# The rotated convolution of every image on 32x32 tiles, with ScalarE turning half of the sums back

## The chip, the cores and the metric

The program runs on one core of a Trainium2 chip. The metric is device time in microseconds, from one launch to its end; the reference and the outputs are float32.

## What is computed

A network of four residual layers over x, (4, 256, 64, 64). Layer 0 is a deformable convolution (its samples are gathered rows of a table), layer 1 a grouped 3x3 convolution whose kernels are rotated by an angle that each image gives itself, layer 2 linear attention, layer 3 a quantised grouped convolution. The change touches layer 1 alone:

```python
B, C, H, W = x.shape                       # 4, 256, 64, 64
G, Cg = (base_kernel.shape[0], base_kernel.shape[1])      # 8 groups of 32 channels
pooled = x.mean(axis=(2, 3))
h = jax.nn.relu(pooled @ ap_w1.T + ap_b1)
angles = jnp.tanh(h @ ap_w2.T + ap_b2) * (math.pi / 4)
rot = jax.vmap(jax.vmap(_rotate_one), in_axes=(None, 0))(base_kernel, angles)
w = rot.reshape(B * C, Cg, K, K)
out = jax.lax.conv_general_dilated(x.reshape(1, B * C, H, W), w, ..., feature_group_count=B * G)
m = jax.nn.relu(pooled @ meta_w1.T + meta_b1)
mod = jax.nn.sigmoid(m @ meta_w2.T + meta_b2)
return feat * mod[:, :, None, None]
```

Before the convolution the image is normalised; its result, times `mod`, is added to the image.

## The kernel before

The images are worked off in turn, and each goes through A (first part of layer 0), F (its second part), L1, L2 and, last of all, L3. Images are named b = 0 to 3. A channel image is 128 partitions by 4096 elements, in two halves (k = 0, 1), and is worked in 8 chunks of 512 columns; PSUM `PS` has 8 banks of 128x512.

**The stream.** Layer 0's samples of the next image are fetched while the phases of this image run. A unit is one of 4 groups of one of 32 tiles: GpSimd issues 9 indirect gathers (L482) into one of the 4 slots of `ring`, after a wait on `ring_free`; VectorE multiplies the slot by the weights (TENSOR_TENSOR, L1700), adds up (TENSOR_REDUCE, L1706) and so frees it. At the first unit of a tile VectorE also moves the weights (COPY, L1689). In the program of VectorE the units are laid between the instructions of the phase: `stream.begin(part, gi, i)` takes those of one iteration (2 tiles, that is 8 units, in L1 of images 0 and 1; 1 tile in that of image 2, part "L1 last"; none in that of image 3), `stream.give(1, 4)` lays down a quarter of them, `stream.finish()` the rest. So L1 holds 32, 32, 16 and 0 units. GpSimd runs ahead of VectorE by at most the four slots, from one phase into the next.

**L1 of images 0 to 2.** TensorE builds the rotated kernels (36 products `PS<-cb,params`), VectorE copies them, masked, into a zeroed 128x128 matrix for each tap (`wa_sb`, four copies on L2156; the zeroing, L2111, is done for image 0 only). A loop of 4 iterations then does 2 chunks in each: 18 float32 matmuls 128x128x512 a chunk (9 taps, 2 halves; each shows as two records in the trace) into two banks; VectorE adds the chunk to the image (2 instructions on L2166) and takes its statistics (2 on L2171), with a quarter of the iteration's units ahead of each chunk and one behind. Semaphore `lC` counts chunks that TensorE has done, `lX` those that VectorE has taken; `room(pe, "lX", n)` lets TensorE be two chunks ahead. ScalarE has nothing to do in this loop, and waits at the barrier behind it.

**L1 of image 3**, where no units are left, is packed: the eight groups lie apart on the array, so 16 matmuls of 32x32 run on 16 tiles at a time. A batch n = 0 to 3 (`quad`, `k`) is 4 chunks of one half, 144 matmuls, 288 records. Tile (r, j) writes the sums of rows r to partitions (r + j) % 4 of bank 2j + k, so chunk j comes out turned by j x 32 partitions. VectorE turns it back as it adds: 1, 4, 2 and 4 instructions (L2183), then 4 statistics (L2188).

Of the kernel before, what the change touches and what calls it, by code (L numbers as in the profile page):

```python
# [28 lines left out]
P = 128  # L29
# [106 lines left out]
def network_kernel(nc, x, par, wa, wr, wf, wq, w3, out):  # L136
    ctx = ExitStack()
    with ctx:
# [222 lines left out]
        def packed(n):  # L361

            return START + (B - 1) * CHUNKS + n
# [490 lines left out]
        def _(pe):  # L854
# [211 lines left out]
            def L1(b):  # L1066
# [22 lines left out]
                def l1(i):  # L1089
                    for h in range(2):  # L1090
                        n, c = i * 2 + (b * CHUNKS + h), i * 2 + h
                        room(pe, "lX", n)
                        for k in range(KC):
                            for tap in range(K2):
                                at = R_SIZE + (k * K2 + tap) * P
                                last = mm(PS[:, 2 * h + k, :].rearrange("p (r x) -> p r x", x=W), wseg(wa_sb, at, P),
                                          padded(k, c, tap // 3, tap % 3), tap == 0, tap == K2 - 1)
                        last.then_inc(sem("lC"), 1)

                def l1_packed(quad, k):  # L1100

                    if quad:
                        pe.wait_ge(sem("lX"), packed(k + 1))
                    for tap in range(K2):
                        for j in range(4):
                            for r in range(4):
                                to = (r + j) % 4
                                at = R_SIZE + (k * K2 + tap) * CG
                                rs, os_ = slice(r * CG, (r + 1) * CG), slice(to * CG, (to + 1) * CG)
                                last = mm(rows(PS[os_, 2 * j + k, :]), wa_sb[rs, at:at + CG],  # L1110
                                          padded(k, quad * 4 + j, tap // 3, tap % 3)[rs], tap == 0, tap == K2 - 1,
                                          tile_position=(r * CG, to * CG), skip_group_check=True)
                    last.then_inc(sem("lC"), 1)

                if b < B - 1:
                    loop(l1)
                else:
                    for quad in range(2):
                        for k in range(KC):
                            l1_packed(quad, k)  # L1120
# [184 lines left out]
        def _(act):  # L1305
# [164 lines left out]
            def L1(b):  # L1470
# [19 lines left out]
                barrier()  # L1490
                barrier()
# [182 lines left out]
        def _(dve):  # L1674
# [415 lines left out]
            def L1(b, gi):  # L2090
# [17 lines left out]
                lt = wseg(wa_sb, R_SIZE, KC * K2 * P)  # L2108
                if b == 0:

                    link(vec.memset(lt, 0.0))  # L2111
# [16 lines left out]
                dve.wait_ge(sem("l1_hats"), b + 1)  # L2128
# [20 lines left out]
                sums = PS[:, 2:4, 0:K2 * CG].rearrange("p k (t o) -> p k t o", t=K2)  # L2149
                if b == B - 1:  # L2150
                    last = vec.tensor_copy(lt[:, 0:KC * K2 * CG].rearrange("p (k n) -> p k n", k=KC), PS[:, 2:4, 0:K2 * CG])
                else:
                    lt4 = lt.rearrange("p (k t o) -> p k t o", k=KC, t=K2)
                    for q in range(P // CG):
                        r_ = slice(q * CG, (q + 1) * CG)
                        last = vec.tensor_copy(lt4[r_, :, :, r_], sums[r_])  # L2156
                link(last)
                barrier()

                def l1(i):  # L2160
                    for h in range(2):
                        n, c = i * 2 + (b * CHUNKS + h), i * 2 + h
                        stream.give(1, 4)
                        done(dve, "lC", n)
                        for k in range(KC):
                            last = vec.scalar_tensor_tensor(out=chunk_of(img1, k, c), in0=PS[:, 2 * h + k, :], scalar=mod[:, k:k + 1],  # L2166
                                                            in1=chunk_of(img1, k, c), op0=ALU.mult, op1=ALU.add)
                        last.then_inc(sem("lX"), 1)
                        done(dve, "lX", n)
                        for k in range(KC):  # L2170
                            vec.bn_stats(seg(stats, c * 6 + k * 48, 6), chunk_of(img1, k, c))  # L2171
                        stream.give(1, 4)
                def l1_packed(quad, k):

                    n = quad * KC + k
                    dve.wait_ge(sem("lC"), packed(n + 1))
                    for j in range(4):
                        img = chunk_of(img1, k, quad * 4 + j)
                        width = (P, CG, 2 * CG, CG)[j]
                        for first in range(0, P, width):  # L2180
                            to = slice(first, first + width)
                            at = (first + j * CG) % P
                            last = vec.scalar_tensor_tensor(out=img[to], in0=PS[at:at + width, 2 * j + k, :],  # L2183
                                                            scalar=mod[to, k:k + 1], in1=img[to], op0=ALU.mult, op1=ALU.add)
                    last.then_inc(sem("lX"), 1)
                    dve.wait_ge(sem("lX"), packed(n + 1))
# [3 lines left out]
                if b < B - 1:  # L2190
                    chunks("L1" if gi != B - 1 else "L1 last", gi, 0, l1)
                else:
                    for quad in range(2):
                        for k in range(KC):
                            l1_packed(quad, k)
# [385 lines left out]
```

## Time and profile before

| | |
|---|---|
| median of 3 runs | 8428.0 us (8407.72 to 8446.78) |
| profiled execution, own time | 8406.53 us |
| its span, first to last instruction | 8404.7 us |
| mean granted TensorE clock | 0.711 |
| busy: TensorE, VectorE, ScalarE, GpSimd | 3952.7, 5151.7, 1232.6, 4440.0 us |
| loop of L1, image 0 | 2719.82 to 3094.4: 374.6 us |
| image 1 | 4593.96 to 4969.5: 375.5 us |
| image 2 | 6447.44 to 6654.8: 207.3 us |
| image 3, packed | 7853.30 to 7907.0: 53.7 us |

A loop's start is the first instruction of its phase behind the barrier, its end the first one behind the next barrier. All times inside a phase are us from the span's start.

### The profile page before, as it was taken

The numbers are of one execution on the slowest core, as the hardware profiler recorded it, in microseconds if no ns is written. First come the engines' busy times: TensorE is split into PE (matmuls) and PEld (weight loads), VectorE is DVE, ScalarE is ACT, GpSimd is POOL, SyncE is SP. The second block draws the span as 40 slices with busy tenths as digits, with TensorE's granted clock in tenths as the row PEclk, the third lists the DMA queues.
The fourth block names the chain that finished last, engine by engine and source line by source line (L and its number), as shares of the span: only waits on it lengthen the run. The fifth ranks groups of instructions, "written<-read, shape, count | busy, mean of one in ns | idle before, by whom it ended". The sixth has DMA issues, their size and how long they took to land.

```text
span 8404.7 us, 44163 instructions
## 1 busy us (share of the span) xinstructions
PE 3952.7 (47%) x11246; PEld 2022.5 (24%) x11246; DVE 5151.7 (61%) x4233; ACT 1232.6 (15%) x1846; POOL 4440.0 (53%) x4684
## 2 busy tenths in 40 slices
PE   6133241341365535442555435442565544428797
PEld 3121121221122213221222113221222222213453
DVE  6667668576566646664666646654666665553556
ACT  1000100001111001111111001111110011112246
POOL 2666656666565655565665655565666555650000
PEclk8566665675687657766787667766787777669899
DMA  4442533534333322244333322244333223441128
GB/s 130 129 128 87 158 113 123 151 109 136 111 107 96 99 85 87 90 153 161 115 96 102 99 81 91 88 159 150 116 113 95 76 89 96 151 149 42 43 99 236
DMA packets 511085, 953.74 MB, mean 113 GB/s; under 512 B 252032, under 2 KB 300928, under 8 KB 494848
## 3 DMA queue, kind: packets, MB, share of 16 engines
q0 software_dynamic: 221184, 604.27, 23.3%
q1 hardware_dynamic: 289792, 348.19, 12.9%
q8 instruction: 47, 0.77, 0.0%
q14 instruction: 62, 0.51, 0.0%
HBM read 791.89 MB, written 160.24 MB: 113 GB/s over the span
## 4 chain that ended last, share of the span: by engine, by line
issue 30%; another core or an unknown queue 26%; DVE 17%; PE 17%; ACT 4%; POOL 3%; DMA 2%; DVEq 1%; SPq 1%; ACTq 0%; POOLq 0%
PE PS L859 16%; DVE ring L1700 6%; DVE dbuf L1706 3%; ACT img L1310 3%; POOL ring L482 3%; DVE PS L1882 1%; DMA img<-d_dram 1%; DVE cb L1767 1%; DVEq L384 1%; DVE img L2067 1%; ACT cb L1310 0%; DVE stats L1762 0%; DVE img L2183 0%; PE PS L1176 0%
## 5 line engine op out<-in xcount | busy, mean ns | idle before, releaser
L482 POOL DMA_INDIRECT ring<-table,idx_stage x4608 | 4422.2, 960 | 3021.7 <-DVE dbuf L1706 1550.4
L1706 DVE TENSOR_REDUCE dbuf<-ring 128x64 f32<-128x2304 f32 x512 | 2071.1, 4045 | 109.6 <-issue 79.8
L859 PE MATMUL PS<-img,wb_sb 128*128 128x512 f32 (+1 forms) x3264 | 1646.0, 665 | 989.4 <-issue 401.9
L1700 DVE TENSOR_TENSOR ring<-ring,PS 128x2304 f32<-128x2304 f32 x480 | 1222.6, 2547 | 119.6 <-DMA ring<-table,idx_stage 101.4
L859 PE MATMUL PS<-img,wa_sb 128*128 (+2 forms) x2908 | 944.3, 635 | 624.2 <-issue 459.7
L859 PEld LDWEIGHTS PS<-img,wb_sb 128*128 128x128 f32 x3264 | 688.3, 215 | 1913.2 <-issue 1692.9
L859 PEld LDWEIGHTS PS<-img,wa_sb 128*128 128x128 f32 (+2 forms) x2908 | 385.2, 166 | 1153.7 <-issue 1123.1
L859 PE MATMUL PS<-wb_sb,img 128*128 128x512 f32 x512 | 344.1, 837 | 518.3 <-ACT cb L1310 221.5
L859 PE MATMUL PS<-wa_sb,cb 128*128 128x256 f32 (+1 forms) x992 | 262.2, 427 | 542.4 <-issue 269.8
L2067 DVE SCALAR_TENSOR_TENSOR img<-PS,params,img 128x512 f32<-128x512 f32 x256 | 179.9, 744 | 507.2 <-ACT img L1310 358.9
L2230 DVE TENSOR_REDUCE sm<-PS 128x16 f32<-128x1024 f32 x64 | 78.3, 1224 | 610.3 <-remote 465.1
L1310 ACT ACTIVATE img<-PS,sm 128x512 f32<-128x512 f32 x384 | 247.2, 680 | 1244.4 <-remote 674.0
L859 PEld LDWEIGHTS PS<-wa_sb,cb 128*128 128x128 f32 x992 | 228.1, 293 | 598.4 <-issue 438.2
L530 POOL MEMSET img<- 128x192 f32 x1 | 0.3, 258 | 659.7 <-DMA o_dram<-img 659.7
L1310 ACT ACTIVATE img<-PS 128x512 f32<-128x512 f32 (+1 forms) x224 | 174.2, 778 | 968.7 <-remote 298.3
L859 PEld LDWEIGHTS PS<-wb_sb,img 128*128 128x128 f32 x512 | 135.5, 277 | 709.5 <-issue 456.6
L859 PE MATMUL PS<-sm,params 128*128 128x4 f32 x28 | 7.7, 350 | 622.2 <-DVE sm L1746 319.0
L990 PE MATMUL PS<-params,img 128*128 128x128 f32 x254 | 61.7, 423 | 504.3 <-DMA img<-d_dram 485.6
L1310 ACT ACTIVATE img<-img 64x512 f32 (+7 forms) x276 | 206.1, 749 | 444.2 <-DVE img L2031 267.5
L2031 DVE SCALAR_TENSOR_TENSOR img<-PS,params,img 128x512 f32 (+1 forms) x64 | 45.0, 744 | 343.6 <-remote 305.1
L859 PE MATMUL PS<-cb,img 128*128 128x256 f32 x1024 | 239.0, 382 | 2.0 <-ACT img L1310 2.0
L1206 PE MATMUL PS<-params,img 128*128 128x128 f32 x512 | 106.3, 387 | 268.9 <-issue 217.8
(253 smaller groups left out, 3305.4 us busy)
## 6 DMA issues: line engine op xcount, KB each, us to landing
ring<-table,idx_stage POOLq DMA_INDIRECT x4608
table<-cb SPq DMA_DIRECT2D x64, 512.0 KB
img<-y_dram SPq DMA_DIRECT2D x64, 512.0 KB
q_dram<-img SPq DMA_DIRECT2D x32, 1024.0 KB
img<-q_dram SPq DMA_DIRECT2D x28, 1024.0 KB
img<-in_x SPq DMA_DIRECT2D x8, 2048.0 KB
y_dram<-cb SPq DMA_DIRECT2D x64, 256.0 KB
img<-in_x SPq DMA_DIRECT2D x32, 512.0 KB
```

What stands on the lines that cost most here:

```text
L384: self.eng.drain().then_inc(sem(self.me + "_phase"), 1)
L482: nc.gpsimd.indirect_dma_start(out=ring[:, g, p * CORNERS * GC:(p + 1) * CORNERS * GC], out_offset=None, in_=tab[b], in_offset=bass.Indire ...
L859: return nc.tensor.matmul(o, l, r, start=start, stop=stop, **kw)
L990: last = nc.tensor.transpose(PS[:, 2 * h + k, s * P:(s + 1) * P], sums[:, k * P:(k + 1) * P], v("ident"))
L1206: last = nc.tensor.transpose(PS[:, m, s * P:(s + 1) * P], QS[:, s * HID + m * P:s * HID + (m + 1) * P], v("ident"))
L1310: return nc.scalar.activation(o, i, f, **kw)
L1700: last = vec.tensor_tensor(rg, rg, weights.unsqueeze(2).to_broadcast([P, n, GC]), ALU.mult)
L1706: vec.tensor_reduce(dbuf[:, j, g * GC:(g + 1) * GC], ring[:, g, :].rearrange("p (k c) -> p c k", c=GC), AX_X, ALU.add).then_inc(sem("ring_ ...
L1767: return vec.scalar_tensor_tensor(out=o, in0=i, scalar=SLOPE, in1=i, op0=ALU.mult, op1=ALU.max)
L1882: last = vec.scalar_tensor_tensor(out=acc, in0=src, scalar=w_, in1=acc, op0=ALU.mult, op1=ALU.add)
L2067: last = vec.scalar_tensor_tensor(out=i2[6 + q % 2][:, half], in0=PS[:, 2 * (q % 2) + j, :], scalar=v("fc1_b", 2 * q + j), in1=i2[4 + q % ...
L2230: link(vec.tensor_reduce(mx, q3, AX_X, ALU.max))
```

## The change

All four images take the packed form. Images 0 to 2 use four banks (bank j, the same for both halves), so batch n + 1 may start only when batch n has been taken (`packed(b, n)` on `lX`); image 3 keeps bank 2j + k, with batch n two behind. ScalarE turns chunks 1 and 3 of each batch back, 8 ACTIVATE Copy of 32x512 from `PS` into `cb`; VectorE adds chunks 0 and 2 from `PS` (1 and 2 instructions), then waits for `l1_hats` and adds the two in `cb`. VectorE's weight copy becomes one instruction, the zeroing goes, and the loops are written out, with constants in their waits. Half of the iteration's units lie ahead of a batch, half behind it.

```diff
+        def packed(b, n):
+            return START + b * PAIRS + n
+        turned_back = {1: cb[:, 0:CHUNK], 3: cb[:, CHUNK:2 * CHUNK]}
+        def l1_turned(b, n):
+            return b * (PAIRS + 1) + (n + 2)
+        def l1_bank(b, j, k):
+            return 2 * j + k if b == B - 1 else j
...
                 def l1_packed(quad, k):
-                    if quad:
-                        pe.wait_ge(sem("lX"), packed(k + 1))
+                    if b < B - 1:
+                        pe.wait_ge(sem("lX"), packed(b, quad * KC + k))
+                    elif quad:
+                        pe.wait_ge(sem("lX"), packed(b, k + 1))
...
-                                last = mm(rows(PS[os_, 2 * j + k, :]), wa_sb[rs, at:at + CG],
+                                last = mm(rows(PS[os_, l1_bank(b, j, k), :]), wa_sb[rs, at:at + CG],
...
-                if b < B - 1:
-                    loop(l1)
-                else:
-                    for quad in range(2):
-                        for k in range(KC):
-                            l1_packed(quad, k)
+                for quad in range(2):
+                    for k in range(KC):
+                        l1_packed(quad, k)
...
                 barrier()
+                for n in range(PAIRS):
+                    k = n % KC
+                    act.wait_ge(sem("lX"), packed(b, n))
+                    act.wait_ge(sem("lC"), packed(b, n + 1))
+                    for j, dst in turned_back.items():
+                        for to in range(0, P, CG):
+                            at = (to + j * CG) % P
+                            last = A_(dst[to:to + CG], PS[at:at + CG, l1_bank(b, j, k), :], ACT.Copy)
+                    last.then_inc(sem("l1_hats"), 1)
                 barrier()
...
-                if b == 0:
-
-                    link(vec.memset(lt, 0.0))
...
-                        last = vec.tensor_copy(lt4[r_, :, :, r_], sums[r_])
+                link(vec.tensor_copy(lt.rearrange("p (k n) -> p k n", k=KC), PS[:, 2:4, 0:K2 * CG]))
...
+                    dve.wait_ge(sem("lC"), packed(b, n + 1))
+                    for j, width in ((0, P), (2, 2 * CG)):
...
+                            vec.scalar_tensor_tensor(out=img[to], in0=PS[at:at + width, l1_bank(b, j, k), :],
+                                                     scalar=mod[to, k:k + 1], in1=img[to], op0=ALU.mult, op1=ALU.add)
+                    dve.wait_ge(sem("l1_hats"), l1_turned(b, n))
+                    for j, src in turned_back.items():
+                        img = chunk_of(img1, k, quad * 4 + j)
+                        last = vec.scalar_tensor_tensor(out=img, in0=src, scalar=mod[:, k:k + 1], in1=img,
+                                                        op0=ALU.mult, op1=ALU.add)
                     last.then_inc(sem("lX"), 1)
...
+                for n in range(PAIRS):
+                    stream.begin(part, gi, n)
+                    stream.give(1, 2)
+                    l1_packed(n // KC, n % KC)
+                    stream.finish()
+                stream.ended(part, gi)
                 barrier()
```

VectorE's queue in the loop of images 0 and 1, before: one of the two chunks of an iteration, from its weight copy on (`ring` and `dbuf` are the stream's, `lC` is TensorE's word that the chunk is done).

```order
L1689 COPY PS<-wt 128x144
L1690 REGISTER_ALU
L1693 REGISTER_ALU [waits wt_moved]
L1700 TENSOR_TENSOR ring<-ring,PS 128x2304 [waits gathered0]
...
L1706 TENSOR_REDUCE dbuf<-ring 128x64 [waits weighted]
L356 REGISTER_ALU
L2166 ISA [waits lC]
L2166 SCALAR_TENSOR_TENSOR img<-PS,sm,img 128x512
L2166 ISA
L2166 SCALAR_TENSOR_TENSOR img<-PS,sm,img 128x512
L2171 ISA [waits lX]
L2171 BN_STATS stats<-img 128x6
```

The same queue of the changed kernel, from the fourth unit ahead of batch 0 to the first behind it (the lines have moved: L1707 and L1713 are the unit's).

```order
L1713 TENSOR_REDUCE dbuf<-ring 128x64 [waits weighted]
L2165 SCALAR_TENSOR_TENSOR img<-PS,sm,img 128x512 [waits lC]
L2165 SCALAR_TENSOR_TENSOR img<-PS,sm,img 64x512 x2
L2170 SCALAR_TENSOR_TENSOR img<-cb,sm,img 128x512 [waits l1_hats]
L2170 SCALAR_TENSOR_TENSOR img<-cb,sm,img 128x512
L2175 BN_STATS stats<-img 128x6 [waits lX]
L2175 BN_STATS stats<-img 128x6 x3
L1696 COPY PS<-wt 128x144
L1707 TENSOR_TENSOR ring<-ring,PS 128x2304 [waits gathered0,wt_moved]
```

Where two units and then one chunk stood, four units stand ahead of four chunks; between two batches VectorE now does eight units, and what it waits for is a batch of 288 records and ScalarE's copies.

TensorE's queue of the changed kernel in L1 of image 0, whole.

```order
L869 MATMUL PS<-img,wa_sb 32x512 [waits dve_phase,lX,act_phase,sp_phase]
L869 MATMUL PS<-img,wa_sb 32x512 x143
L869 MATMUL PS<-img,wa_sb 32x512 [waits lX]
L869 MATMUL PS<-img,wa_sb 32x512 x143
L869 MATMUL PS<-img,wa_sb 32x512 [waits lX]
...
L869 MATMUL PS<-sm,params 128x4 [waits wb_loaded,dve_phase,gn_moments,act_phase,sp_phase]
```

Here stood a loop with 18 matmuls of 128x512 behind each wait for `lX`; the wait now stands ahead of every batch of 144, and lets TensorE no batch ahead.

## Rows read from the trace of the kernel before

**Rows 1.** The page: the span, and three costly groups (busy, mean ns; idle before).

```profile
span 8404.7 us, 44163 instructions
...
L482 POOL DMA_INDIRECT ring<-table,idx_stage x4608 | 4422.2, 960 | 3021.7 <-DVE dbuf L1706 1550.4
L1706 DVE TENSOR_REDUCE dbuf<-ring 128x64 f32<-128x2304 f32 x512 | 2071.1, 4045 | 109.6 <-issue 79.8
...
L1310 ACT ACTIVATE img<-PS,sm 128x512 f32<-128x512 f32 x384 | 247.2, 680 | 1244.4 <-remote 674.0
```

**Rows 2.** Timeline, VectorE, image 0's loop: start, busy, instruction, idle before.

```profile
2719.82 0.31 DVE L1689 COPY PS<-wt 128x144 f32 x1 [0.58 <-ACTq L384]
...
2803.13 1.41 DVE L2166 SCALAR_TENSOR_TENSOR img<-PS,sm,img 128x512 f32 x2 [36.40 <-remote]
2804.68 1.29 DVE L2171 BATCH_NORM_STATS2 stats<-img  x2
2805.89 2.54 DVE L1700 TENSOR_TENSOR ring<-ring,PS 128x2304 f32<-128x2304 f32 x1
...
3007.66 1.41 DVE L2166 SCALAR_TENSOR_TENSOR img<-PS,sm,img 128x512 f32 x2 [50.66 <-remote]
...
3094.43 0.60 DVE L1740 BATCH_NORM_AGGREGATE sm<-stats 128x2 f32<-128x48 f32 x2 [0.75 <-issue]
```

**Rows 3.** Timeline, GpSimd, the same loop: where runs of gathers start and end.

```profile
2727.86 0.94 POOL L482 DMA_INDIRECT ring<-table,idx_stage  x1 [35.24 <-DVE dbuf L1706]
...
2794.21 0.95 POOL L482 DMA_INDIRECT ring<-table,idx_stage  x1 [0.30 <-issue]
2813.37 0.95 POOL L482 DMA_INDIRECT ring<-table,idx_stage  x1 [18.21 <-DVE dbuf L1706]
...
3017.84 0.95 POOL L482 DMA_INDIRECT ring<-table,idx_stage  x1 [24.10 <-DVE dbuf L1706]
```

**Rows 4.** Timeline, TensorE, the same loop, around the first stall.

```profile
2749.72 7.89 PE L859 MATMUL PS<-img,wa_sb 128*128 x18
...
2759.58 0.59 PE L859 MATMUL PS<-img,wa_sb 128*128 x1 [1.97 <-issue]
...
2800.88 5.54 PE L859 MATMUL PS<-img,wa_sb 128*128 x8 [0.39 <-issue]
```

**Rows 5.** Timeline, VectorE: first and last instruction, loops of images 1, 2.

```profile
4593.96 0.31 DVE L1689 COPY PS<-wt 128x144 f32 x1 [0.58 <-ACTq L384]
...
4969.48 0.60 DVE L1740 BATCH_NORM_AGGREGATE sm<-stats 128x2 f32<-128x48 f32 x2 [0.75 <-issue]
...
6447.44 0.31 DVE L1689 COPY PS<-wt 128x144 f32 x1 [0.56 <-ACTq L384]
...
6654.78 0.60 DVE L1740 BATCH_NORM_AGGREGATE sm<-stats 128x2 f32<-128x48 f32 x2 [1.32 <-issue]
```

**Rows 6.** Timeline, TensorE, phase A2 of image 0: small matmuls, first gathers running.

```profile
138.98 0.25 PE L859 MATMUL PS<-wa_sb,cb 128*128 128x108 f32 x1
...
155.78 0.34 PE L859 MATMUL PS<-wa_sb,cb 128*128 128x108 f32 x1 [2.46 <-issue]
```

**Rows 7.** Timeline, ScalarE, the same place.

```profile
159.38 2.85 ACT L1310 ACTIVATE cb<-PS,sm 128x512 f32<-128x512 f32 x4 [36.06 <-remote]
```

**Rows 8.** Timeline, TensorE: the kernel products of image 2, gathers running.

```profile
6419.07 5.44 PE L859 MATMUL PS<-cb,params 128*128 128x288 f32 x12 [37.14 <-DVE cb L2145]
```

**Rows 9.** Timeline, TensorE: image 3's packed L1, its first three batches.

```profile
7853.30 28.07 PE L859 MATMUL PS<-img,wa_sb 32*32 32x512 f32 x864 [1.00 <-ACTq L384]
```

**Rows 10.** Timeline, VectorE: zeroing (image 0), weight copies (2), packed L1 (3).

```profile
2698.83 1.98 DVE L2111 MEMSET wa_sb<- 128x2304 f32 x1 [0.55 <-DVE sm L2107]
...
6443.83 3.05 DVE L2156 COPY wa_sb<-PS 32x576 f32<-32x576 f32 x4 [13.82 <-remote]
...
7863.18 8.38 DVE L2183 SCALAR_TENSOR_TENSOR img<-PS,sm,img 128x512 f32<-128x512 f32 x11 [10.08 <-PE PS L859]
7871.59 2.47 DVE L2188 BATCH_NORM_STATS2 stats<-img 128x6 f32<-128x512 f32 x4
```

More of the change, by code:

```diff
@@ L1087, in L1 @@
                 barrier()
[L1089 to L1092, printed above, removed]
-                        for k in range(KC):
[L1094 to L1098, printed above, removed]
                 def l1_packed(quad, k):
-                    if quad:
-                        pe.wait_ge(sem("lX"), packed(k + 1))
+                    if b < B - 1:
+                        pe.wait_ge(sem("lX"), packed(b, quad * KC + k))
+                    elif quad:
+                        pe.wait_ge(sem("lX"), packed(b, k + 1))
                     for tap in range(K2):
@@ L1113, in l1_packed @@
                     last.then_inc(sem("lC"), 1)
-                if b < B - 1:
-                    loop(l1)
-                else:
-                    for quad in range(2):
-                        for k in range(KC):
-                            l1_packed(quad, k)
+                for quad in range(2):
+                    for k in range(KC):
+                        l1_packed(quad, k)
                 barrier()
@@ L2127, in L1 @@
                 last.then_inc(sem("l1_uv"), 1)
-                dve.wait_ge(sem("l1_hats"), b + 1)
+                dve.wait_ge(sem("l1_hats"), l1_turned(b, -1))
                 for t in (BX, AY):
@@ L2148, in L1 @@
                 dve.wait_ge(sem("l1_products"), (b + 1) * (K2 + 2))
[L2149 to L2155, printed above, removed]
-                        last = vec.tensor_copy(lt4[r_, :, :, r_], sums[r_])
-                link(last)
-                barrier()
[L2160 to L2172, printed above, removed]
+                link(vec.tensor_copy(lt.rearrange("p (k n) -> p k n", k=KC), PS[:, 2:4, 0:K2 * CG]))
+                barrier()
                 def l1_packed(quad, k):
                     n = quad * KC + k
-                    dve.wait_ge(sem("lC"), packed(n + 1))
-                    for j in range(4):
+                    dve.wait_ge(sem("lC"), packed(b, n + 1))
+                    for j, width in ((0, P), (2, 2 * CG)):
                         img = chunk_of(img1, k, quad * 4 + j)
-                        width = (P, CG, 2 * CG, CG)[j]
                         for first in range(0, P, width):
@@ L2182, in l1_packed @@
                             at = (first + j * CG) % P
-                            last = vec.scalar_tensor_tensor(out=img[to], in0=PS[at:at + width, 2 * j + k, :],
-                                                            scalar=mod[to, k:k + 1], in1=img[to], op0=ALU.mult, op1=ALU.add)
+                            vec.scalar_tensor_tensor(out=img[to], in0=PS[at:at + width, l1_bank(b, j, k), :],
[5 more added lines that the diff above has]
+                                                        op0=ALU.mult, op1=ALU.add)
                     last.then_inc(sem("lX"), 1)
-                    dve.wait_ge(sem("lX"), packed(n + 1))
+                    dve.wait_ge(sem("lX"), packed(b, n + 1))
                     for j in range(4):
                         vec.bn_stats(seg(stats, (quad * 4 + j) * 6 + k * 48, 6), chunk_of(img1, k, quad * 4 + j))
[L2190 to L2195, printed above, removed]
+                part = "L1" if gi != B - 1 else "L1 last"
+                if gi is not None:
+                    weights_for(gi)
+                for n in range(PAIRS):
[4 more added lines that the diff above has]
+                stream.ended(part, gi)
                 barrier()
```

4 lines of the change are left out of this document (1 added, 3 removed).

## The prediction

> **What bounds the kernel now.** I read the page's groups first, then the timelines of GpSimd and VectorE in the four L1 loops, and TensorE's last. On the page GpSimd's gathers are busy 4422.2 us and idle 3021.7 before them, 1550.4 of it until VectorE frees a slot [rows 1]. So the stream sets the time of the loops that carry it, and a loop's length is its gathers plus the gaps between their runs. From 2727.86 to 2795.16 stand 54 gathers, 1.25 us each; a unit of nine takes 11.25 us [rows 3]. The loop of image 0 starts at 2719.82 and ends at 3094.4 [rows 2]. Four of its 32 units lie in the ring at its start, so 28 are gathered in it: 8.0 (start to the first gather) + 28 x 11.25 = 315 + gaps of 18.2 and 24.1 [rows 3] + 8.3 (last gather to the loop's end: landing, unit) = 373.6, against 374.6 seen.
>
> Both gaps come from one thing. VectorE stands 36.40 us before the chunk of 2803.13, and 50.66 before that of 3007.66 [rows 2]; the ring fills, GpSimd stops, and only then does the chunk come: 8.0 us after the last gather's end at 2795.16 in the first case [rows 2, 3]. TensorE shows why. At 2749.72 it did 18 records in 7.89 us; from 2759.58 its records come singly, with "issue" before them, 16 in the 41.3 us to 2800.88, 2.6 us apart; at 2800.88, 5.7 us after the gathers stopped, it is quick again [rows 4]. So while gathers flow, beginning some 13 to 25 us after a run starts, something lets TensorE finish only a record in about 2.65 us.
>
> The change depends on whether that price is per record or per column. In A2 of image 0 matmuls of only 108 columns stand 2.4 us apart in the mean (138.98 to 155.78, seven steps) with 0.25 to 0.34 us of work in each [rows 6], under the first gathers, and ScalarE gets their result after 36.06 us of waiting [rows 7]. That code is written out, without a loop. So I take it per record. Against it stand the 36 products of image 2: 12 records of 288 columns in 5.44 us under gathers [rows 8], all of them in hand at 6443.83 [rows 10], 24.8 us for 36, that is 0.69 us each.
>
> **The change, images 0 and 1.** Without gathers a packed record costs 28.07 / 864 = 0.0325 us and a batch of 288 takes 9.4 [rows 9]; the plain loop has 72 records for as many sums, at 0.44 each. The change thus makes four records of one, each a thirteenth as long (0.0325 to 0.44). Batch 0 is done at 9.4 from the loop's start, hidden behind four units (a unit: 2.54 + 4.05 + the step between, 6.65 [rows 1, 2]); VectorE takes it at 27 to 31. Batch 1 may start only then, 23 us into a run of gathers, in the slow stretch. VectorE comes for it eight units later, at 31 + about 75 = 106. By 2.65 a record that is some 30 done and 60 started, not 288. VectorE stands; the ring fills when 12 units have been gathered, at 8 + 12 x 11.25 = 143; GpSimd stops. Then follow, in a row: 5.7 until TensorE is quick, 7.4 for the other 228 records, ScalarE's 8 copies at 0.68 (128x512 from PSUM, [rows 1]; the 32x512 form is not in the trace: 0.6 to 0.7) 5.4, VectorE's two adds from `cb` 1.4 and four statistics 2.5 [rows 2, 10], a unit with its weight copy and the step to the gather 7.7: a gap of 30.1 where 18.2 stood. (The same sum for the old gap: 8.0 + 1.4 + 1.3 + 6.6 + 0.8 = 18.1.) Three adds from `PS` lie beside ScalarE's copies.
>
> Batch 2 may start as soon as batch 1 is taken, ahead of the next run of gathers, and needs 9.4 of the 20 or so quick microseconds: in time. Batch 3 starts eight units later, in the slow stretch: VectorE stands again. All but four units have been gathered by then, at 8 + 315 + the first gap, and behind the stop follow 22.4 (5.7 + 7.4 + 5.4 + 1.4 + 2.5), the four units of the ring 26.6, and 0.8. The second gap of before was 5.9 longer than the first, after a longer run of gathers [rows 3]; for the run before batch 3 (180 us) I add 5.9, for that before batch 1 (135 us) half, 3.0. Loop: 8.0 + 315 + 33.1 + 5.9 + 49.8 = 411.8, against 374.6 and 375.5 [rows 2, 5]: **+37.2 and +36.3**. What GpSimd has gathered ahead for L2 is worth nothing: there it gets its slots no earlier than that phase's own work lets it.
>
> **Image 2** has 16 units, four an iteration, 12 of them gathered in the loop. Batch 1 starts at about 17.5, 9.5 us into the run, and needs 9.4: at the edge of the slow stretch. Late, batches 1 and 3 stall: 8 + 14 x 11.25 (two units for the phase behind fill the ring) + 30.1 + 22.4 + 13.3 + 0.8 = 232.1. In time, only batch 2 stalls, and its loop ends at 120.5 (stop) + 22.4 + four units 26.6 + the taking of batch 3 6.1 + two units 13.3 + 0.4 = 189.3. Before 207.3 [rows 5]. The ends are +24.8 and -18.0, nothing decides between them, and I take the middle: **+3.4**.
>
> **Image 3** has no gathers. VectorE was the bound: 8.38 + 2.47 a batch [rows 10]. Now four batches of TensorE (37.8) bound it, plus 0.5, 5.4, 1.4 and 2.5: from 7853.3 to 7901, where the table has 7907.0 as the end: **-6.0**.
>
> **Ahead of the loops** four copies of 3.05 become one of them, 0.76: -2.3 in each of images 0 to 2, nothing else being at work there, **-6.9**. The zeroing (1.98, [rows 10]) is worth 0 to 2.0, as the products start behind later work; I take **-1.5**. ScalarE's copies cost nothing where batches are in time, since it idles; under the stalls they are in the sum. Constants in place of register waits save 0.1 us here and there in VectorE's queue, behind the gathers.
>
> Sum: 37.2 + 36.3 + 3.4 - 6.0 - 6.9 - 1.5 = **+62.5**, on the profiled execution's own 8406.5: 8469. That execution is at the low end of the runs shown (8407.7 to 8446.8, median 8428.0), so I keep to it and say 8470, knowing that the median may lie up to 20 higher.
>
> The Trainium skill has a rule on the notification block ("NOTIFIC — the notification-queue block", section "Overflow: three behaviours, one of which stalls the engine"): its internal pipeline holds the producers back rather than lose a record. A price per record instead of per column is what such a thing would look like; the trace agrees in the 2.4 us of 108-column matmuls, but nothing in it shows the block itself.
>
> **Rivals.**
> *The gathers don't slow packed batches enough* (30 in 100). Should the price go by the work in a record, as [rows 8] lean to (0.69 at 288 columns under gathers against 0.0325 x a few), a batch must be done in the 75 us between its start and VectorE's coming: the point is 0.26 us a record. Then all gaps go: images 0 and 1 take 8.0 + 315 + 8.3 = 331.3 (-43.3, -44.2), image 2 8 + 12 x 11.25 + 8.3 = 151.3 (-56.0), and with -14.4 for the rest the time is 8249. For it speaks that TensorE's work in the loop shrinks from 288 x 0.44 = 126 to 38 us; against it, [rows 6].
> The Trainium skill, "TensorEngine Tiling (Array Packing)", section "PSUM Bottleneck", says that after tiling it is the copy out of PSUM that may bind, and to use ScalarE and VectorE for it. By that rule the change does all that is needed and this rival is the outcome; in image 3 the trace agrees (VectorE's 10.9 a batch against 9.4).
> *Milder slow stretch* (13): at 0.69 a record, 162 records are done when GpSimd stops, still not 288, so the stalls stand, but each is about 3.3 shorter, and without the late signals another 3: 5.5 stalls by 6 us off, 8437, no change that can be told.
> *Batch 2 stalls too* (12), if the slow stretch comes at once with the new run, or the 9.4 grow: three more gaps of 30 and the worse end for image 2: 8580.
> *Forecast* (42), its own range 8440 to 8500. The last 3 in 100 are for what I don't see.
>
> **Numbers.** Within 0.5% (42 us, about what a measurement of this kernel can tell from none) lie the milder stretch and the forecast's low edge. Slower: 0.38 of the forecast's 0.42, batch 2's 0.12 and a little. The range runs from the first rival's 8249, less a little, to 8510, and leaves out mainly the 8580.
>
> **What would show it.** In the loop of image 0: GpSimd with one gap near 33 us, near 143 from the loop's start, and a second stop near 356; VectorE's adds behind "remote" twice, each followed by a wait on ScalarE of 3 to 5 us; TensorE's packed records single, 2 to 3 us apart, from some 13 to 25 us after a run of gathers starts, and quick 6 us after it stops; loop 400 to 415. Image 3: VectorE waiting on TensorE, end near 48 from the start. Wrong if TensorE shows 144-matmul batches of 10 to 60 us under gathers: then the first rival holds, and VectorE never stands.

## The result, and the profile after

The changed kernel took 8509.0 us (median of 5 runs, 8470.2 to 8535.1), the kernel before 8409.9 beside it (5 runs, 8407.7 to 8446.8): ratio 1.0103, 95% interval 1.007 to 1.0136. Forecast was 8470 from the sum, range 8240 to 8510. So it is 1% slower, clear of the spread of its runs, and the time lies 1 us inside the upper end of the range. Two later comparisons on other chips gave 1.0119 (1.0077 to 1.0161) and 1.0089 (1.007 to 1.0108); one run of the kernel before beside the first of them, 8972.97 us at a granted clock of 0.579, is left out as disturbed.

The page of the changed kernel: GpSimd's gathers, the packed group, and what VectorE's adds waited for.

```profile
span 8533.2 us, 48722 instructions
...
L492 POOL DMA_INDIRECT ring<-table,idx_stage x4608 | 4413.1, 958 | 3149.2 <-DVE dbuf L1713 1679.5
...
L869 PE MATMUL PS<-img,wa_sb 32*32 32x512 f32 (+2 forms) x5500 | 857.6, 707 | 833.5 <-issue 644.0
...
L1308 ACT ACTIVATE cb<-PS 32x512 f32<-32x512 f32 (+1 forms) x160 | 107.9, 675 | 1394.9 <-PE PS L869 664.4
...
L2165 DVE SCALAR_TENSOR_TENSOR img<-PS,sm,img 64x512 f32<-64x512 f32 (+1 forms) x48 | 36.0, 749 | 384.9 <-PE PS L869 288.6
```

Beside [rows 1] the gathers are as busy as before, and GpSimd is idle 128 us longer before them, the whole of it until VectorE frees a slot (1550.4 to 1679.5). The profiled execution's span grew by 128.5; from the weight copies to the next phase L1 of images 0 to 2 takes 432.7, 416.9 and 255.7 where 378.2, 379.1 and 210.9 stood (+137), and image 3 7.7 less.

TensorE's timeline of the changed kernel, loop of image 0 (single records between are left out).

```profile
2729.27 10.35 PE L869 MATMUL PS<-img,wa_sb 32*32 32x512 f32 x288 [1.20 <-DVEq L394]
2759.62 3.85 PE L869 MATMUL PS<-img,wa_sb 32*32 32x512 f32 x37 [19.99 <-issue]
2764.12 1.01 PE L869 MATMUL PS<-img,wa_sb 32*32 32x512 f32 x1 [0.65 <-issue]
2766.92 1.01 PE L869 MATMUL PS<-img,wa_sb 32*32 32x512 f32 x1 [1.79 <-issue]
...
2884.58 1.01 PE L869 MATMUL PS<-img,wa_sb 32*32 32x512 f32 x1 [1.09 <-issue]
...
2888.07 9.02 PE L869 MATMUL PS<-img,wa_sb 32*32 32x512 f32 x204 [0.24 <-issue]
2903.47 12.98 PE L869 MATMUL PS<-img,wa_sb 32*32 32x512 f32 x288 [6.38 <-DVE img L2170]
2970.68 3.88 PE L869 MATMUL PS<-img,wa_sb 32*32 32x512 f32 x41 [54.23 <-issue]
```

Batch 0 takes 10 us. Batch 1 starts 22 us into a run of gathers: 37 records go, and then they come singly, mostly 2.1 to 3.5 us apart (2.7 in the mean), for 120 us, in packed matmuls as in the plain ones of [rows 4]. The granted clock is 1.00 in 2729 to 2739 and 0.50, the 1.2 GHz level, in 2764 to 2872; a single record shows 1.01 us there in place of 0.59, but the 1.1 to 2.5 us of "issue" ahead of it are idle time, which the clock does not explain. Batch 2, ahead of the next run, takes 13, at a granted clock of 0.79. Batch 3 repeats batch 1. GpSimd and VectorE in the same loop:

```profile
2737.25 0.94 POOL L492 DMA_INDIRECT ring<-table,idx_stage  x1 [25.45 <-DVE dbuf L1713]
...
2871.40 0.95 POOL L492 DMA_INDIRECT ring<-table,idx_stage  x1 [0.30 <-issue]
2913.80 0.94 POOL L492 DMA_INDIRECT ring<-table,idx_stage  x1 [41.45 <-DVE dbuf L1713]
...
3093.15 0.95 POOL L492 DMA_INDIRECT ring<-table,idx_stage  x1 [0.30 <-issue]
3140.73 0.94 POOL L492 DMA_INDIRECT ring<-table,idx_stage  x1 [46.63 <-DVE dbuf L1713]
```

```profile
2729.21 0.31 DVE L1696 COPY PS<-wt 128x144 f32<-128x144 f32 x1 [0.34 <-DVE wa_sb L2153]
...
2897.13 2.28 DVE L2165 SCALAR_TENSOR_TENSOR img<-PS,sm,img 128x512 f32<-128x512 f32 x3 [61.38 <-PE PS L869]
2902.00 1.41 DVE L2170 SCALAR_TENSOR_TENSOR img<-cb,sm,img 128x512 f32<-128x512 f32 x2 [2.60 <-ACT cb L1308]
...
3124.29 2.28 DVE L2165 SCALAR_TENSOR_TENSOR img<-PS,sm,img 128x512 f32<-128x512 f32 x3 [66.80 <-PE PS L869]
...
3160.81 0.60 DVE L1747 BATCH_NORM_AGGREGATE sm<-stats 128x2 f32<-128x48 f32 x2 [1.41 <-issue]
```

Against [rows 2, 3]: the runs of gathers are 135.1 and 180.3 us long, as worked out; VectorE stands 61 and 67 us where it stood 36 and 51; the gap in GpSimd's work is 41.5 where 18.2 stood. What was not foreseen is the time from the last gather to TensorE's quick records: 2872.35 to 2888.07, 15.7 us, and 3094.10 to 3115.74, 21.6.

In images 1 and 2 batch 0 stalls as well. TensorE in image 2, where runs of gathers stand from 6563.40 to 6585.57, 6609.24 to 6653.95 and 6676.49 to 6766.81:

```profile
6555.40 14.79 PE L869 MATMUL PS<-img,wa_sb 32*32 32x512 f32 x224 [1.10 <-DVEq L394]
6570.59 3.38 PE L869 MATMUL PS<-img,wa_sb 32*32 32x512 f32 x8 [0.39 <-issue]
...
6588.27 4.59 PE L869 MATMUL PS<-img,wa_sb 32*32 32x512 f32 x41 [0.39 <-issue]
6599.27 13.84 PE L869 MATMUL PS<-img,wa_sb 32*32 32x512 f32 x269 [6.40 <-DVE img L2170]
6613.50 1.07 PE L869 MATMUL PS<-img,wa_sb 32*32 32x512 f32 x5 [0.39 <-issue]
```

The quick stretch ends 7 and 4 us into a run of gathers, with 224 and 269 records of the batch done. Batch 0 was not quick enough to be out of the way: the kernel products ahead of it ran under gathers at a granted clock of 0.50 (6530 to 6555), and in its first 8 us, up to the gathers, the clock was 0.65 and 181 records went; in image 0, at 1.00, all 288 took 10.4. VectorE stands three times:

```profile
6592.90 2.28 DVE L2165 SCALAR_TENSOR_TENSOR img<-PS,sm,img 128x512 f32<-128x512 f32 x3 [23.77 <-PE PS L869]
...
6660.13 2.28 DVE L2165 SCALAR_TENSOR_TENSOR img<-PS,sm,img 128x512 f32<-128x512 f32 x3 [31.82 <-remote]
...
6787.51 2.28 DVE L2165 SCALAR_TENSOR_TENSOR img<-PS,sm,img 128x512 f32<-128x512 f32 x3 [57.41 <-PE PS L869]
```

The second of these is no wait for records: TensorE's last one of batch 1 ended at 6625.20, and VectorE took the batch 35 us later, 6 us after the gathers had stopped. The same stands twice in image 1, where VectorE and ScalarE start within 0.1 us of each other, long after TensorE has ended:

```profile
4725.70 1.01 PE L869 MATMUL PS<-img,wa_sb 32*32 32x512 f32 x2 [0.39 <-issue]
4781.20 2.28 DVE L2165 SCALAR_TENSOR_TENSOR img<-PS,sm,img 128x512 f32<-128x512 f32 x3 [9.52 <-issue]
4781.26 4.78 ACT L1308 ACTIVATE cb<-PS 32x512 f32<-32x512 f32 x8 [74.58 <-issue]
...
5022.25 2.28 DVE L2165 SCALAR_TENSOR_TENSOR img<-PS,sm,img 128x512 f32<-128x512 f32 x3 [22.16 <-issue]
```

By the trace those batches were done 54.5 and 65.5 us before they were taken (4726.71 and 4956.74). So under gathers not only TensorE's records come late, but also the word that a finished batch is done.

Image 3's packed loop, VectorE (its first two batches, and the end):

```profile
7998.61 2.28 DVE L2165 SCALAR_TENSOR_TENSOR img<-PS,sm,img 128x512 f32<-128x512 f32 x3 [10.10 <-PE PS L869]
8003.41 1.41 DVE L2170 SCALAR_TENSOR_TENSOR img<-cb,sm,img 128x512 f32<-128x512 f32 x2 [2.52 <-ACT cb L1308]
...
8007.62 2.28 DVE L2165 SCALAR_TENSOR_TENSOR img<-PS,sm,img 128x512 f32<-128x512 f32 x3 [0.28 <-PE PS L869]
...
8034.70 0.60 DVE L1747 BATCH_NORM_AGGREGATE sm<-stats 128x2 f32<-128x48 f32 x2 [0.22 <-SPq L392]
```

VectorE now waits for TensorE, by 0.3 us, a batch is 9.0 to 9.1 us long where it was 10.9 [rows 10], and the loop 46.0 (7988.72 to 8034.70) where 53.7 stood.

### The profile page after: what moved, and what is told of

Same layout as the page of the kernel before. It is cut to its first block, busy times and chain, and to the rows that moved or that the text cites. A ratio compares the mean times of both kernels' runs of the same rounds, so it can differ in the third digit from the quotient of the medians.

```text
span 8533.2 us, 48722 instructions
## 1 busy us (share of the span) xinstructions
PE 3850.6 (45%) x13838; PEld 1939.0 (23%) x13838; DVE 5131.9 (60%) x4211; ACT 1308.5 (15%) x1974; POOL 4430.5 (52%) x4684
## 4 chain that ended last, share of the span: by engine, by line
issue 28%; another core or an unknown queue 26%; PE 20%; DVE 18%; ACT 4%; DMA 1%; DVEq 1%; SPq 1%; POOL 1%; ACTq 0%; POOLq 0%
PE PS L869 19%; DVE ring L1707 6%; DVE dbuf L1713 4%; ACT img L1308 3%; DVE PS L1889 1%; ACT cb L1308 1%; POOL ring L492 1%; DVE cb L1774 1%; DVEq L394 0%; DMA img<-d_dram 0%; DVE stats L1769 0%; DVE img L2074 0%; PE PS L1174 0%; SPq L758 0%
## 5 line engine op out<-in xcount | busy, mean ns | idle before, releaser
L492 POOL DMA_INDIRECT ring<-table,idx_stage x4608 | 4413.1, 958 | 3149.2 <-DVE dbuf L1713 1679.5
L1713 DVE TENSOR_REDUCE dbuf<-ring 128x64 f32<-128x2304 f32 x512 | 2070.2, 4043 | 76.4 <-issue 27.3
L1707 DVE TENSOR_TENSOR ring<-ring,PS 128x2304 f32<-128x2304 f32 x480 | 1223.0, 2548 | 119.7 <-DMA ring<-table,idx_stage 104.3
L869 PE MATMUL PS<-img,wa_sb 32*32 32x512 f32 (+2 forms) x5500 | 857.6, 707 | 833.5 <-issue 644.0
L869 PEld LDWEIGHTS PS<-img,wa_sb 32*32 32x32 f32 (+2 forms) x5500 | 309.8, 127 | 1351.0 <-issue 1229.3
L1308 ACT ACTIVATE cb<-PS 32x512 f32<-32x512 f32 (+1 forms) x160 | 107.9, 675 | 1394.9 <-PE PS L869 664.4
L1000 PE MATMUL PS<-params,img 128*128 128x128 f32 x254 | 61.7, 423 | 519.3 <-DMA img<-d_dram 510.2
L869 PE MATMUL PS<-sm,params 128*128 128x4 f32 x28 | 7.7, 351 | 607.6 <-DVE sm L1753 331.3
L2165 DVE SCALAR_TENSOR_TENSOR img<-PS,sm,img 64x512 f32<-64x512 f32 (+1 forms) x48 | 36.0, 749 | 384.9 <-PE PS L869 288.6
```

The source lines that it names most:

```text
L492: nc.gpsimd.indirect_dma_start(out=ring[:, g, p * CORNERS * GC:(p + 1) * CORNERS * GC], out_offset=None, in_=tab[b], in_offset=bass.Indire ...
L869: return nc.tensor.matmul(o, l, r, start=start, stop=stop, **kw)
L1000: last = nc.tensor.transpose(PS[:, 2 * h + k, s * P:(s + 1) * P], sums[:, k * P:(k + 1) * P], v("ident"))
L1308: return nc.scalar.activation(o, i, f, **kw)
L1707: last = vec.tensor_tensor(rg, rg, weights.unsqueeze(2).to_broadcast([P, n, GC]), ALU.mult)
L1713: vec.tensor_reduce(dbuf[:, j, g * GC:(g + 1) * GC], ring[:, g, :].rearrange("p (k c) -> p c k", c=GC), AX_X, ALU.add).then_inc(sem("ring_ ...
```

## The experiments

The theory: under gathers TensorE ends a record per 2 to 3 us, and that, not the packed form's own work, costs the time. Rival: the packed form costs something of its own (copies, banks, code). The runs fell on five chips of two kinds: on three of them (called quick here) the kernel before, the same program, took 6797 to 6801 us, on two (slow) 8345 to 8446, as beside the result. The times compared are always of one chip.

**e1 and e2: other order of the same instructions** (kernel before 6798.3 beside them). e1 takes three batches ahead of the units (the diff); e2 takes two ahead, the third behind one unit and the last behind three more.

```diff
+                first = 3 if gi is not None else PAIRS
+                for n in range(first):
+                    l1_packed(n // KC, n % KC)
                 for n in range(PAIRS):
                     stream.begin(part, gi, n)
                     stream.give(1, 2)
-                    l1_packed(n // KC, n % KC)
+                    if n == 1 and first < PAIRS:
+                        l1_packed(first // KC, first % KC)
                     stream.finish()
```

> The changed kernel with the units of images 0 to 2 moved: VectorE takes batches 0, 1 and 2 first, with no unit ahead of them, and batch 3 in the middle of the second iteration; the instructions are the same. Theory (TensorE ends a record per 2.6 us under gathers, from some 13 us after a run starts until 6 to 22 us after it stops, the longer the run the longer; all the rest is quick): at the loop's start the gathers stand, so the three batches are done at their quick price, one behind the other since they share banks, 16 us each, and batch 3 starts ahead of the next run: no packed record is slow, VectorE never stands for TensorE behind the first 51 us, GpSimd has no gap inside the loop. Loop of image 0: 51 + 7.7 + 315 + 8.3 = 382 (changed kernel 431.6, kernel before 374.6), of image 2 51 + 7.7 + 135 + 8.3 = 202 (254.6, 207.3); in all about 8509 - 50 - 34 - 52 = 8375 to 8400. Rival (what costs is the packed form's own work, on whatever engine, or the fetching of its written-out code): 4 batches cost the same wherever they stand; the loops stay near 430 and the time near 8509.

> As the one with three batches first, but only batches 0 and 1 stand ahead of the units; batch 2 is taken behind one unit and batch 3 behind three more. Theory: batch 2 runs while VectorE does its first unit, batch 3 starts some 7 us into the run of gathers and needs about 10: just inside the 13 quick microseconds. If inside, image 0's loop is 35 + 7.7 + 315 + 8.3 = 366, image 2's 186, and the time is about 40 us under that with three first (8335 to 8360); if not, VectorE stands once more for batch 3 and each loop gets a gap of 25 to 35. Rival as there: no change against the changed kernel.

Measured: e1 6931.8 us (ratio 1.0196, 1.0179 to 1.0213), e2 6893.6 (1.014, 1.0123 to 1.0157). TensorE in e2, image 0, with gathers running from 2268.56:

```profile
2224.02 9.90 PE L869 MATMUL PS<-img,wa_sb 32*32 32x512 f32 x288 [1.10 <-DVEq L394]
2240.33 11.50 PE L869 MATMUL PS<-img,wa_sb 32*32 32x512 f32 x288 [6.40 <-DVE img L2170]
2258.21 11.13 PE L869 MATMUL PS<-img,wa_sb 32*32 32x512 f32 x288 [6.38 <-DVE img L2170]
2275.72 12.54 PE L869 MATMUL PS<-img,wa_sb 32*32 32x512 f32 x288 [6.38 <-DVE img L2170]
```

Every batch is quick, and the loops of image 0 are 388 (e1) and 375 us (e2) from TensorE's start, near the 382 and 366 worked out. But on such a chip these orders can only lose: the loop without a stall is 332 us (e3 below), and GpSimd stands for 56 and 38 us at its head. So the absolute forecasts missed, as their base did not hold; what was seen is that a packed batch under gathers is quick on such a chip (12.5 us for batch 3).

**e3: each 512-column matmul of the kernel before as two of 256.** The two halves' sums are interleaved in one bank here, and the output is not the reference's; **e7** does the halves in turn, and its output is.

```diff
-                            for tap in range(K2):
+                            for half in range(2):
+                                for tap in range(K2):
+                                    rr = slice(half * 4, half * 4 + 4)
```

> The kernel before, with each matmul of 512 columns in L1 of images 0 to 2 made as two of 256: twice the records (576 an image), the same columns and sums. Theory (price per record under gathers): a chunk of 72 records isn't finished in the time that 36 just were; three stalls an image in place of two, gaps of 24 to 31 each; loops of images 0 and 1 from 375 to 400 to 435, image 2's longer by 10 to 30; time up by 80 to 150. Rival (price per column or per us of work): the loops stay within 5 us of 374.6, 375.5 and 207.3, the time within 0.3%.

> The kernel before with each 512-column matmul of L1, images 0 to 2, made as two of 256, the nine taps of one half and then those of the other: 576 records an image, the same columns and sums. Where the kernel before takes some 8410 us here: theory (a price per record under gathers) expects single records 2 to 3 us apart as before, three stalls an image, loops of images 0 and 1 of 400 to 435 (374.6, 375.5), time up by 50 to 150; rival (a price per column) expects loops within 5 us and records 1.0 to 1.4 us apart. Where it takes some 6800 both expect no change, as in e3.

Measured: 6799.0 (beside 6798.3) and 6794.9 (beside 6798.2), both on chips of the quick kind, so they don't tell record from column under slow stretches. They do give the floor. The page of e3:

```profile
span 6797.1 us, 46323 instructions
...
L482 POOL DMA_INDIRECT ring<-table,idx_stage x4608 | 4427.4, 961 | 1413.1 <-issue 1376.0
```

The gathers are as long as in [rows 1], but nothing is lost to waits for VectorE: they are issued back to back, 4608 x 1.25 = 5760 us, and the rest is ahead of them and behind. Loops of images 0 to 2: 332.3, 342.9, 163.3, where the first rival had 331.3, 331.3 and 151.3: image 0's is met, the other two are 12 us longer.

**e4, e8, e10: plain matmuls in the changed kernel's batches** (the masked weight copies and the zeroing are back; the diff shows the matmul alone).

```diff
-                                last = mm(rows(PS[os_, l1_bank(b, j, k), :]), wa_sb[rs, at:at + CG], ...
+                            last = mm(rows(PS[:, l1_bank(b, j, k), :]), wseg(wa_sb, R_SIZE + (k * K2 + tap) * P, P), ...
```

> The changed kernel's order, banks, copies by ScalarE and units, but with plain 128x128 matmuls (36 a batch, 72 records, 31 us quick) in place of the packed ones; the masked weight copies and the zeroing are back. Theory A (it is the coarse step, four chunks with none ahead, that turns a stall of one chunk into one of a batch): in the 75 us that VectorE needs to come for batch 1 some 30 records are done, not 72, so batches 1 and 3 stall until the gathers stop as in the changed kernel; loop of image 0 425 to 445 (changed kernel 431.6). Theory B (it is the fourfold number of records alone): a batch of 72 is nearly done when VectorE comes, the gaps are those of before (18 to 25) and the loop is 380 to 395. In both image 3 gets longer by about 90 us, since its loop has no gathers and plain matmuls take 126 us there.

> The kernel of e4 again: plain 128x128 matmuls in the changed kernel's batches of four chunks, none ahead. Where the kernel before takes some 8410 us: theory A (the coarse step does the harm) expects the loop of image 0 at 425 to 445; theory B (the fourfold number of records does) at 380 to 395. Where it takes some 6800: 333, 344 and 175 us as in e4.

> The kernel of e4 and e8 once more, in case this call gets a chip with slow stretches (kernel before near 8410 us). It has the records of the kernel before and the grain, the order of units and the single banks of the changed one; image 3's loop is known to be 83 us longer than before in it. Theory A (the coarse step does the harm: a stall ends only when a whole batch is done and taken): loops of images 0 and 1 as in the changed kernel, 405 to 445, and the time 8410 + 83 + 60 to 140 = 8555 to 8635. Theory B (the number of records does it: something drains a fixed number of them per us under gathers, here or later): loops nearer to 375 and the time 8410 + 83, within 40. Where the kernel before takes some 6800: 6899 as in e4 and e8.

Measured: 6899.4, 6899.6 and 6910.7, each beside 6798 to 6799, each on a quick chip: image 3 83 us longer, image 2's loop 175, the others 332 to 345. Whether the coarse grain or the number of records does the harm on a slow chip is open: all three fell on quick ones.

**e5 and e6: the changed kernel and e2's order side by side** (kernel before 8422.9).

> The changed kernel as it is, beside the kernel before, on whatever chip this call gets. In the last four runs the kernel before took 6798 us, not 8410, and no record of TensorE stood 2 to 3 us from the next under gathers: there the slow stretches were missing. Theory (the slow stretches, not the packed form's work, made the change slower): if the kernel before takes some 6800 here, the loops of images 0 to 2 are bound by gathers alone and equally long in both kernels, and only image 3's loop (-7.7) and the shorter weight copies (up to -8) are left: ratio 0.997 to 1.001. If it takes some 8410, the slow stretches are there and the ratio is 1.005 to 1.016 again. Rival (the packed form's own cost, in copies, banks or code fetched, makes it slower): ratio 1.005 or more in both.

> The order with batches 0 and 1 ahead of the units once more. Where the kernel before takes some 6800 us, GpSimd's standing still while two batches are taken costs 30 us in each of three loops, as in e2 (+95). Where it takes some 8410, theory: loops of images 0 and 1 360 to 400, of image 2 180 to 215, time 8320 to 8400, under both kernels; rival: as the changed kernel.

Measured: e5 8510.3 (ratio 1.0119), L1 432.4, 406.2 and 255.1 us long. e6 8513.1 in its one run: L1 407.1, 401.8 and 207.1, that is 78 us less in the three, with all else the same program. Image 0 still has one stall of 31 us; its loop is 406 us from TensorE's start where 360 to 400 was forecast, and the time missed its 8320 to 8400. The time in all did not fall. It came back behind: from L1's end to the next weight copy e6 takes 46, 21 and 42 us more. These three are rough, as the same instructions up to the first weight copy differ too, by 20 us between e6 and e5 (2693.42 and 2713.07). GpSimd at the first chunk of L2 in image 0, e6 and then e5:

```profile
3179.99 0.94 POOL L492 DMA_INDIRECT ring<-table,idx_stage  x1 [35.86 <-DVE dbuf L1713]
```

```profile
3193.18 0.95 POOL L492 DMA_INDIRECT ring<-table,idx_stage  x1 [22.15 <-DVE dbuf L1713]
```

In e6 gathers ran from 2816.53 to 3144.13 with no stop above 2.1 us, and this result of L2 came to VectorE only after 37.47 us of waiting (6.51 in e5):

```profile
3167.14 1.23 DVE L2229 TENSOR_REDUCE sm<-PS 128x16 f32<-128x1024 f32 x1 [37.47 <-remote]
```

From the loop's end to GpSimd's release are 79.5 us in e6 (3100.5 to 3180.0) and 47.7 in e5 (3145.5 to 3193.2). So the 25 us by which L1 of image 0 was shorter are gone, and 7 more, at L2's first chunk. The forecast that fewer stalls in L1 make the kernel faster did not come true; in image 0 the stall moved to the next place that needs a result. Images 1 and 2 were not followed that far, and e6 is a single run beside four of e5 that span 8498 to 8547.

**e9: gathers spaced.** GpSimd waits ahead of gathers 2, 4, 6 and 8 of a unit for those before.

```diff
+                    if p in (2, 4, 6, 8):
+                        pool.wait_ge(sem(f"gathered{g}"), t * (16 * K2) + (16 * K2 * b * TILES + 16 * p))
+                        pool.sem_inc(sem("unit_begun"), 1)
```

> The changed kernel, but GpSimd waits ahead of every second gather of a unit until the gathers before it have landed, so that at most two are under way and the gathers come more slowly; the time in all is longer (some 512 x 8 us more). Where the kernel before takes some 8410 us: if the slow stretches come from the number of gathers in a stretch of time (a backlog that grows while they are issued faster than something drains), TensorE's records stay quick, batches take 10 to 15 us wherever they start and VectorE never stands for them. If they come from gathers being under way at all, single records 2 to 3 us apart stay.

Measured: 11715.4 beside 6798.2, a quick chip, where every batch was quick anyway. It says nothing on the cause of the slow stretches, which stays open.

**e11 and e12: the changed kernel, and the change in image 3 alone.**

> The changed kernel once more, for a chip without slow stretches (kernel before near 6800 us). Theory: there the loops of images 0 to 2 are as long as in the kernel before (332, 343, 163 us in e3 and e7), bound by the gathers, and what is left is image 3's loop (-7.7) and the single weight copy in place of four (0 to -2.3 in each of three images): -8 to -15 us, ratio 0.9978 to 0.9990. Rival (the packed form costs something of its own): loops of images 0 to 2 longer by 10 us or more each, ratio above 1.002. Where the kernel before takes some 8410: ratio 1.007 to 1.016 as twice before.

> The kernel before, with the change in image 3 alone: ScalarE turns chunks 1 and 3 back there, and VectorE adds with 5 instructions in place of 11; images 0 to 2 stay as they were. No instruction is added where gathers run, so on either kind of chip: image 3's loop 46 in place of 53.7, time 7 to 8 us under the kernel before (ratio 0.9988 to 0.9992), on a chip with slow stretches within the scatter of its runs.

```diff
+                if b == B - 1:
+                    for n in range(PAIRS):
...
+                                last = A_(dst[to:to + CG], PS[at:at + CG, 2 * j + k, :], ACT.Copy)
...
+                    dve.wait_ge(sem("l1_hats"), B + n + 1)
```

A chip of the slow kind again. e11: 8449.1 beside 8365.5, ratio 1.0089. e12: 8351.5, ratio 0.9982 (0.9962 to 1.0001); its loops of images 0 to 2 are 373.6, 375.3 and 207.7, as before, and image 3's L1 from the weight copy on is 47.0 where 54.6 stood, as in the changed kernel. The 7.6 us are seen in the trace; in the time no difference from none can be told. So in image 3, where no gathers run, the packed form with ScalarE's copies costs nothing of its own, and e1 and e2 show its batches quick in images 0 to 2 on a quick chip: both speak against the rival. e11's L1 is 432.5, 405.5 and 253.5 us long, so the stalls come again in each of three profiles of the changed kernel. On no quick chip was the changed kernel itself timed.

## Why the prediction was right, and where its sizes were off

The way the change went, and the stalls that make it slower, were foreseen. The size was not: the sum gave +62.5, the medians beside each other differ by +99, and the time is inside the range by 1 us of 8510. That it still fell inside is in part luck: image 0's recovery (17 us) and image 2 (44 us) were 61 us too small, where the range left 40 above the 8470, and the profiled execution itself took 8535.

- **What bounds L1** (gathers plus gaps): borne out. Without stalls image 0's loop has 332.3 us in e3 where 331.3 was worked out.
- **The price of a record under gathers**: packed records stood 2.7 us apart in the mean, as plain ones do. So batches 1 and 3 stalled in image 0, batch 2 did not, and the runs of gathers between have the lengths foreseen. That it goes by the record and not the column still rests on the rows of A2; e3 and e7 could not test it.
- **When the slow stretch comes** was misread. The prediction has it begin "some 13 to 25 us after a run starts". In its own [rows 4] TensorE is quick until 2757.6, 30 us after the run's start, and in the next run, which starts at 2813.37, until 2880, 67 us:

```profile
2834.11 18.11 PE L859 MATMUL PS<-img,wa_sb 128*128 x36 [12.24 <-issue]
2868.21 11.80 PE L859 MATMUL PS<-img,wa_sb 128*128 x21 [15.99 <-issue]
2882.22 0.59 PE L859 MATMUL PS<-img,wa_sb 128*128 x1 [2.21 <-issue]
```

  Counted in the traces, TensorE had put out much the same number of records since the run's start each time: 68 and 76 here, 67 to 75 in the four runs of images 1 and 2. In the changed kernel it was 34 to 77, in 4 to 73 us. A count fits better than a time. By it a batch of 288 stalls when it has more than that left as gathers start: batch 0 of image 2 had 107 left and stalled, batch 2 of image 0 some 30 and did not. No run was made to test this. It also takes the weight from [rows 8]: only 36 records (18 matmuls of two records) went since that run of gathers began at 6393.31, too few for the slow stretch.
- **The recovery** was mis-sized. The sum had 5.7 + 3.0 and 5.7 + 5.9 us from the last gather to quick records; they were 15.7 and 21.6. I took the 5.9 from the difference of two gaps, but there the chunk that VectorE waited for was nearly done, and came while TensorE was still slow: TensorE's own timeline of the kernel before is quick only at 3015.22, 21.5 after the last gather's end at 2993.73:

```profile
3013.13 1.01 PE L859 MATMUL PS<-img,wa_sb 128*128 x1 [3.20 <-issue]
3015.22 5.03 PE L859 MATMUL PS<-img,wa_sb 128*128 x6 [1.08 <-issue]
```

  A batch of 288 has to wait for that. This is 7 + 10 of the 19.8 us by which image 0's loop (431.6) passed its 411.8; most of the rest is the end of the batches, 9.0 us for 204 records and 8.5 for 194 where 7.4 stood for 228. ScalarE's copies and the adds were right (8.8 against 9.3).
- **Image 2** was the term furthest off: +47.3 (254.6 against 207.3) for +3.4, beyond even its bad end, +24.8. The sum had batch 0 done in 9.4 us and out of the way, at the quick price of [rows 9], and weighed only when batch 1 would start. Batch 0 itself stalled: 181 records were done when the gathers began, at a granted clock of 0.65, and the slow stretch came 7 us later. With the late word of batch 1 and the stall of batch 3 VectorE stood 23.8, 31.8 and 57.4 us, where it had stood 10.0, 28.5 and 38.1. Image 1 paid for batch 0 too (32.21 us of VectorE's time), and its 415.8 is near the 411.8 by other terms than those foreseen: its waits are 32, 10, 68 and 22 us, not two of some 65. In e5 and e11 the same loop took 405.1 and 404.4.
- **Image 3**: -7.7 for -6.0. **Ahead of the loops**: the span's +128.5 less the loops' +136.9 (57.0 + 40.3 + 47.3 - 7.7) leaves -8.4, the very -6.9 - 1.5; but other stretches vary by more than that from run to run, so it is no proof.
- **The first rival** (no stalls) describes the quick chips: no packed batch is slow there. The rule on the PSUM bottleneck (the Trainium skill, "TensorEngine Tiling (Array Packing)", section "PSUM Bottleneck") fits image 3, where sharing the copy-out with ScalarE moved the bound from VectorE to TensorE; where gathers ran on a slow chip, TensorE's records and signals bound and the rule did not decide.

The +62.5 of the sum stands against +128.5 in the profiled execution and +99 between the medians; beside e5 and e11 the medians differ by +87 and +84.

## What to carry to other kernels

Four times as many instructions, each a thirteenth as long, gain nothing where the price is per instruction; look in the trace for stretches in which small instructions stand as far apart as large ones, before splitting a step. A stall taken out under such a stretch can come back at the next place that needs a result, as e6 showed once, so count the whole iteration, not the loop. And where a step's result is wanted as one large batch, the wait lasts until the whole batch is done: read the recovery from the engine's own rows, not from the consumer's. Compare also when the producer ended with when the consumer started: between them stood up to 66 us.

## What the runs showed of the hardware

One program took 8345 to 8447 us on some chips and 6797 to 6801 on others, with gathers of the same length (0.96 us; 4422 us in all on a slow one, 4427 in e3 on a quick one). On the slow ones TensorE, once gathers had run a while, put out a record per 2.1 to 3.5 us, whether plain or packed, and three finished batches of the changed kernel were taken 35 to 66 us after TensorE's last record of them. The time from the last gather to quick records grew with the run ahead of it: 3.8 us after 45 (image 2, 6519.66 to 6523.42), 5.1 to 6.3 after 67, 15.7 after 135, 21.5 and 21.6 after 180. That looks like a backlog that fills under gathers and is filled further by TensorE's own records (quick for 29 to 67 us and 67 to 76 records from the run's start in plain code, for 4 to 7 us and 34 to 43 records where a packed batch was under way as the gathers began).

Such a backlog would agree with the Trainium skill, "NOTIFIC — the notification-queue block", section "Overflow: three behaviours, one of which stalls the engine", by which the block holds its producers back rather than lose a record inside it. No run here shows that block. Each time on record comes with a profile of the same execution, so no run shows either whether the slow stretches are there without one. What makes one chip slow and another quick is open.
